# Two routings of a two-layer mixture-of-experts kernel: one-hot operands laid out with the token tile outermost

## The reference

```
# layer 0: 4 experts, each token goes to its best 2
probs = jax.nn.softmax(xf @ router_w + router_b, axis=-1)
top_p, top_i = jax.lax.top_k(probs, 2)
gates = zeros(T, e).at[arange(T)[:, None], top_i].add(top_p / sum(top_p))
out = einsum('te,etd->td', gates, expert_out)
# layer 1: 8 experts, each token goes to its best 1
route = jax.nn.sigmoid(x @ Wr + br)
max_ind, max_prob = argmax(route, axis=1), max(route, axis=1)
out = sum over e of (max_ind == e) * (gelu(x @ W1[e]) @ W2[e]), times max_prob
```

## Time and profile before

| | |
|---|---|
| median of 3 runs | 1730.97 us (1727.98 to 1731.4) |
| the profiled execution | 1730.75 us, its span 1729.0 us |
| mean granted TensorE clock | 0.928 |
| PE, DVE, ACT, POOL busy | 1521.6, 1123.6, 905.8, 1217.6 us |
| routing 0 stands at | about 414 to 437 us |
| routing 1 stands at | about 1486 to 1502 us |

### The profile page before, as it was taken

The page is one execution under the profiler, slowest core; times in us unless marked ns, Lnnn a source line. Parts: engine busy times, 40 slices in busy tenths (PEclk is TensorE's granted clock), DMA queues, the critical chain, the costliest instruction groups (busy, mean ns, idle before and its releaser), DMA issues.

```text
span 1729.0 us, 38207 instructions
## 1 busy us (share of the span) xinstructions
PE 1521.6 (88%) x13596; PEld 1140.2 (66%) x13596; DVE 1123.6 (65%) x1786; ACT 905.8 (52%) x2305; POOL 1217.6 (70%) x1024
## 2 busy tenths in 40 slices
PE   6799999986899999999999967777887767699998
PEld 5466665655788888888888843333333226599998
DVE  7888989887343433333445557999999998533333
ACT  6678787843343444343444345545555446354553
POOL 4757777732476676676778627999999996366664
PEclk9899999995799999999999977989999887599999
DMA  6014444418344445545465460011111255388885
GB/s 220 20 41 131 130 145 128 128 37 318 82 116 106 120 104 118 123 100 122 120 171 155 100 215 23 1 31 32 30 42 43 92 176 175 138 264 251 262 264 152
DMA packets 148049, 217.34 MB, mean 126 GB/s; under 512 B 48904, under 2 KB 108576, under 8 KB 142752
## 3 DMA queue, kind: packets, MB, share of 16 engines
q1 hardware_dynamic: 115296, 132.26, 23.7%
q0 software_dynamic: 32576, 82.63, 19.9%
HBM read 143.23 MB, written 71.61 MB: 124 GB/s over the span
## 4 chain that ended last, share of the span: by engine, by line
PE 58%; POOL 20%; DVE 9%; issue 5%; DMA 4%; ACT 1%; POOLq 0%; DVEq 0%; ACTq 0%; SPq 0%
PE ps L832 54%; POOL BIG L2575 17%; DVE BIG L1426 4%; DMA BIG<-HB,BIG 3%; PE ps L953 1%; DVE BIG L2059 1%; PE ps L1134 1%; POOL BIG L2760 1%; POOL BIG L2759 1%; DVE bnst L1433 1%; POOL XD L2749 1%; PE ps L1203 1%; DMA XD<-BIG 1%; ACT BIG L2108 1%; POOL BIG L2737 1%
## 5 line engine op out<-in xcount | busy, mean ns | idle before, releaser
L832 PE MATMUL ps<-BIG 128*128 128x256 f16 (+9 forms) x11168 | 1224.3, 284 | 125.0 <-DVE BIG L2037 49.2
L832 PEld LDWEIGHTS ps<-BIG 128*128 128x128 f16 (+3 forms) x11168 | 936.2, 100 | 383.3 <-DVE BIG L2037 76.3
L2575 POOL TENSOR_TENSOR BIG<-BIG 128x256 f16<-128x256 f32 (+7 forms) x550 | 730.4, 1457 | 211.4 <-ACT BIG L2108 200.1
L2108 ACT ACTIVATE BIG<-BIG 128x512 f16<-128x512 f32 (+3 forms) x527 | 318.0, 662 | 233.2 <-DVE BIG L1426 176.2
L1426 DVE TENSOR_TENSOR BIG<-BIG 128x512 f16<-128x512 f32 (+10 forms) x347 | 259.8, 758 | 209.5 <-ACT BIG L2108 165.0
L2108 ACT ACTIVATE BIG<-ps 128x64 f32<-128x64 f32 (+7 forms) x663 | 232.1, 424 | 194.6 <-PE ps L1134 108.0
L1426 DVE TENSOR_TENSOR BIG<-ps,BIG 128x512 f32<-128x512 f32 (+3 forms) x389 | 284.8, 809 | 14.5 <-PE ps L832 13.1
L1426 DVE TENSOR_TENSOR BIG<-BIG,ps 128x512 f32<-128x512 f32 (+2 forms) x147 | 94.9, 645 | 187.4 <-PE ps L832 168.1
L2059 DVE TENSOR_REDUCE BIG<-BIG 128x160 f32<-128x2560 f32 x64 | 186.0, 2906 | 0.0
L2749 POOL DMA_INDIRECT XD<-BIG x67 | 113.2, 1690 | 85.9 <-DVE BIG L1943 82.1
L2737 POOL DMA_INDIRECT BIG<-HB,BIG x106 | 109.7, 1035 | 50.6 <-issue 27.0
(11 more groups left out here) (176 smaller groups left out, 1025.4 us busy)
## 6 DMA issues: line engine op xcount, KB each, us to landing
WD<-BIG SPq DMA_DIRECT2D x80, 256.0 KB
BIG<-in_v SPq DMA_DIRECT2D x32, 512.0 KB
BIG<-in_w SPq DMA_DIRECT2D x24, 512.0 KB
BIG<-WD SPq DMA_DIRECT2D x32, 384.0 KB, 7.9
HB<-BIG SPq DMA_DIRECT2D x64, 128.0 KB, 2.5
WG<-BIG SPq DMA_DIRECT2D x32, 256.0 KB
BIG<-WD SPq DMA_DIRECT2D x16, 512.0 KB, 5.2
XD<-X SPq DMA_DIRECT2D x32, 128.0 KB, 2.4
```

The lines of the kernel that those rows point to most:

```text
L832: return e.matmul(o, lhsT, rhs, start=start, stop=stop, skip_group_check=True)
L2108: return e.activation(o, i, ACT.Copy)
L2575: return e.tensor_tensor(o, a, b, op)
```

## The change

Three ring buffers change their shape: the token tile, until now the innermost index, becomes the outermost. `S1` goes from [128, 8] to [8, 128], `A1` and `AP` from [2, NS, 8] to [8, 2, NS]. Each matmul now reads its 128 weights per partition and its 134 or 78 moving columns from adjacent addresses; until now two neighbours lay 8 elements (16 bytes) apart. The engines that write these buffers still go through the elements in the old order, with the eight token tiles innermost; the helper `by_tile` turns the output view, so the element after the next one written lies a whole row away (128 elements for `S1`, 2 x NS for `A1` and `AP`). `A0`, `lane8` and `tile8` and the other inputs keep their layout. Sizes, counts, waits and the order of instructions stay.

```diff
+def by_tile(ap):
+    return ap.rearrange("p r n -> p n r")
...
-                self.S1 = late.ring(4, 128, 8, dt=f16) if l else over.ring(3, 128, 8, dt=f16)
-                self.AP = late.ring(4, 2, NS, 8, dt=f16) if l else None
+                self.S1 = late.ring(4, 8, 128, dt=f16) if l else over.ring(3, 8, 128, dt=f16)
+                self.AP = late.ring(4, 8, 2, NS, dt=f16) if l else None
...
-                self.A1 = over.ring(3, 2, NS, 8, dt=f16)
+                self.A1 = over.ring(3, 8, 2, NS, dt=f16)
...
-                            m = mm(m_.mp, m_.S1[n % len(m_.S1)][:, :, r], m_.A1[n % 3][:, :, :, r], n == 0 and r == 0,
+                            m = mm(m_.mp, m_.S1[n % len(m_.S1)][:, r], m_.A1[n % 3][:, r], n == 0 and r == 0,
...
-                            m = mm(m_.pp, m_.S1[n][:, :, r], m_.AP[n][:, :, :, r], n == 0 and r == 0, n == 3 and r == 7)
+                            m = mm(m_.pp, m_.S1[n][:, r], m_.AP[n][:, r], n == 0 and r == 0, n == 3 and r == 7)
...
-                    tt(m_.S1[u % len(m_.S1)], bc(m_.s_lo[:, u // 4, 8 * (u % 4):8 * (u % 4) + 8], 1, 128), m_.lane8, ALU.is_equal).then_inc(s["rt"], 1)
+                    tt(by_tile(m_.S1[u % len(m_.S1)]), bc(m_.s_lo[:, u // 4, 8 * (u % 4):8 * (u % 4) + 8], 1, 128), m_.lane8, ALU.is_equal).then_inc(s["rt"], 1)
...
-                    tt(a1[:, 0], hot, bc(m_.tok[:, ch, g:g + 8], 1, NS), ALU.mult).then_inc(s["rt"], 1)
+                    tt(by_tile(a1[:, :, 0]), hot, bc(m_.tok[:, ch, g:g + 8], 1, NS), ALU.mult).then_inc(s["rt"], 1)
...
-                            tt(m_.AP[u][:, k], m_.A0[u], bc(p[:, 8 * u:8 * u + 8], 1, NS), ALU.mult).then_inc(s["rt"], 1)
+                            tt(by_tile(m_.AP[u][:, :, k]), m_.A0[u], bc(p[:, 8 * u:8 * u + 8], 1, NS), ALU.mult).then_inc(s["rt"], 1)
...
-                    e.activation(m_.A1[u % 3][:, 1], m_.A0[u % len(m_.A0)], ACT.Copy, scale=pcol[:, 0:1]).then_inc(s["a1_a"], 1)
+                    e.activation(by_tile(m_.A1[u % 3][:, :, 1]), m_.A0[u % len(m_.A0)], ACT.Copy, scale=pcol[:, 0:1]).then_inc(s["a1_a"], 1)
```

## The result

The changed kernel takes 1797.47 us in the median of its runs, against 1731.18 us for the kernel before in the same comparison: a ratio of 1.0389, 95% interval [1.037, 1.0407]. One run of the changed kernel took 3070.84 us; it stands apart from the other three (1795.81 to 1797.6 us) and is left out. The profiled execution took 1797.34 us with a span of 1795.6 us, 66.6 us more than before. I had forecast 1746 us with a range up to 1759: the sign was right, the time was outside the range.

A forecast was written before the change was run, and what follows sets the result against it. TensorE was taken as busiest (88%), its 64 matmuls on routing 0's path; slower VectorE writes would add 8.6 us in routing 0 and 6.15 in routing 1, +14.8, giving 1746 us, range 1733 to 1759.

The forecast's parts named there:

- What it costs VectorE: Both routings: strided writes cost 1.69 ns per element, bounds 1.05 and 2.33; S1 of 1024 elements 1.88 us, before 0.68.
- Rival 2: VectorE's strided writes: a two-byte write costs a read and a write, 2.33 ns per element; +28 us, 1759; chance 15%.
- TensorE's gain: Matmuls of both routings: packed operands cut a unit of eight to 0.92 us (from 1.97) and 0.54 (from about 1.18).
- (a): Routing 0: first three S1 and GpSimd's four additions take turns, each waiting for the other's running instruction; +3.6 us.
- (b): Routing 0: three pairs of one-hot and token product, 0.83 us apart before, 1.45 after.
- (c): Routing 0, units 3 to 7: period 3.14 us, TensorE needing 0.92 of it and waiting for VectorE.
- (d): End of routing 0: VectorE work that used to hide under TensorE's last units now stands open, 2.0 us.
- Routing 1: Routing of layer 1: line 1860 moves by +5.65 us, AP products add 2.9, the routing as a whole +6.15 us.
- ScalarE: ScalarE's part of 536 elements could grow from 744 ns to about 1.2 us, beside VectorE's 1.9 us, costing nothing.
- The clock: Dense work behind both routings: the clock's rise costs nothing new if it follows the work; at most 2 to 3 us.
- Rival 3: Both routings: VectorE keeps two elements per cycle and TensorE was all that counted; 1724.3 us; chance 7%.

The follow-up runs named there:

- m1: Kernel of single operations alone in different layouts, computing nothing of the reference; VectorE's 1024 two-byte results take 4703 ns at a step of 256 bytes, packed 692.
- e1: Changed kernel with A1 and AP put back as before, so only S1 is turned: 1776.36 us in one run, against 1734.95 for the kernel before.
- e2: Changed kernel with S1 put back as before, so only A1 and AP are turned: 1752.93 us in one run, +18 us.
- e5: Kernel before with only A1 and AP laid out in runs of four token tiles, S1 untouched: 1730.3 us against 1736.72, ratio 0.9967.
- e3: Kernel before with S1, A1 and AP all laid out in runs of four token tiles: 1728.04 us against 1734.95, ratio 0.9963.
- e4: Kernel before with S1, A1 and AP laid out in runs of two token tiles: 1733.55 us against 1736.72, ratio 0.9984.

## Why the prediction was wrong

The step that failed is the one under "What it costs VectorE": "I take 1.69, since TensorE's 16-byte step costs nearly the same per column; both ends are kept." The write costs 4.4 ns per element. Not only the value was wrong: the upper bound, 2.33, was too. I built it from float32 rows of another stride, charged twice, and m1 shows that these rows measure a different thing: a float32 word that hops costs 1.71 ns, a lone two-byte word 4.4. I found no row of a strided two-byte write in the trace of before, so 2.33 was a guess of a mechanism and bounded nothing. Rival 2 named the property that counts (the two-byte size), at half its price and at 15%; its reason, a read and a write back, is not shown: from 4 to 16 bytes the price grows with the step, which two fixed accesses would not give.

- **TensorE's gain.** 1.05 us per unit against 0.92 forecast, 0.70 against 0.54 in routing 1, both with a fixed part that I left out (about 0.15 us for each separated group). Right in kind. That the `S1` half of it is nothing, which e1, e2 and e5 show, I had not seen.
- **(a) Turns with GpSimd.** Right for GpSimd's side only. Its additions, from the groups of that stretch:

```profile
L2580 POOL TENSOR_TENSOR BIG<-BIG 128x268 f32<-128x268 f32 x1 | 4.5, 4452 | 0.1
L2580 POOL TENSOR_TENSOR BIG<-BIG 128x134 f32<-128x134 f32 x1 | 4.3, 4268 | 0.1
```

  They took 0.94 and 0.76 us before, and now each lasts nearly as long as the `S1` beside it. From the first `S1` to line 1827 it is 14.02 us, before 3.28: +10.7 where I had +3.6. But the three `S1` follow one another in 13.91 us, 4.6 each, so they hardly waited for an addition: turns as I had drawn them would have made it 15.4 at this price.
- **(b) Pairs.** TensorE's first groups stand 2.82 us apart (433.65 and 436.47); I had 1.45.
- **(c) Period.** The five groups from 446.29 to 475.28 stand 7.25 us apart; I had 3.14. VectorE's wait for TensorE is gone, as I said.
- **(d) Tail.** Line 1865 starts 1.87 us behind the last product (475.46 to 477.33); I had 2.0.

The stretches add up: 14.0 for the turns, 1.2 for the three conversions, 3 x 2.82, 5 x 7.25 and 1.9 are 61.8 us, where 62.2 were measured. That only says that no stretch is missing. The test of my steps is to put in the prices of m1 (4.70 us for an `S1`, 2.52 for a product of 536): they give 15.4, 1.2, 8.8, 37.2 and 2.0, 64.6 us. So the path and the overlaps of routing 0 were right to 2.4 us, more than half of it the turns, and the price of the write made up nearly all of the miss.

- **Routing 1.** +19.4 at line 1865 against +5.65, by the same price: four units of 4.0 + 1.15 are 20.7, less what TensorE gives back. Behind it, I had the last conversion and the second row fetch end at the same moment, 1507.05, each ready to hold TensorE. With the `AP` products at +8.7 us and not +2.9, the conversion (line 1897) comes last alone, and TensorE waits for it.
- **ScalarE** "costs nothing": in routing 0 that held, though at 2.68 and not 1.2 us, since VectorE's period was longer still.
- **The clock** gave a little over 1 us back, inside its term.
- **Rival 3** fell: below 0.9 ns the sign would have turned. e3 shows that its idea was sound (TensorE's 15.8 us are on the chain, and 5.9 of 6.05 us can be had), but only with writes that stay in runs; in runs of two it is 3.0 us (e4).

## What to carry to other kernels

Before a tile is turned for the engine that reads it, look at how its writer will step through it: the adjacent elements that are written together must stay adjacent, and a run of four two-byte elements was enough for VectorE's full speed here. What step the reader can bear depends on its clock: 8 bytes cost TensorE 1.14 against 1.08 us per unit at 0.50, and 120 against 57 ns per matmul at 1.00 (with both operands at 8 bytes, m1). Turn only the operand that gains by it (here the moving one, not the weights), and only as far as it gains. Where the trace has no row for an operation of this size of element, a bound built from rows of another size is no bound; widen the range by a factor, or measure the one operation first.

## What the runs showed of the hardware

- A two-byte result costs VectorE, with two sources, 0.28 ns per byte of step: 1.30 us for 1024 at 4 bytes, 2.43 at 8, 4.69 at 16 and no more beyond. In runs of two it is 1.03 us, in runs of four 0.69 as if packed. The Trainium skill, "SBUF — State Buffer", section "Door 1: The DMA port swizzle", says that accesses within one 16-byte line run at full bandwidth, so that up to 8 two-byte elements can be stepped over for free. For these writes the runs do not agree: the price begins at 4 bytes, and 16 bytes is where it stops rising.
- GpSimd and ScalarE pay about the same 4.7 us for 1024 at 256 bytes (4734 and 4743), from 2114 and 1056 packed.
- TensorE's moving operand at 16 bytes costs about twice the packed one at a clock of 0.50 (2.07 against 1.08 us per unit, e1 and the changed kernel), while weights at 16 bytes cost 0.03 us. In m1 at 1.00 a packed matmul of 128 columns takes 57 ns, 60 with the moving operand at 4 bytes and 120 with both at 8; with the moving one at 16 bytes it takes more than 200 at either level.
- A long VectorE instruction holds up GpSimd's indirect fetch as well. The first indirect fetch of weights in routing 1, which took 1.14 us before, has in the changed kernel's timeline

```profile
1541.10 4.43 POOL L2798 DMA_INDIRECT BIG<-WG,BIG  x1 [23.64 <-DVE BIG L1431]
```

- In routing 0 the granted clock was 0.50 throughout before, although TensorE was busy for 15.75 of 15.8 us there. With runs of four (e3) it rose to 1.00 in the middle of the routing, for about 3.5 us, and fell back. Two windows of e3, one ahead of the rise and one in it:

```profile
418.00:420.00 2.00, 1.11 (x10) 1.14 (x11) 1.93 (x5) 1.84 (x3) 0.00 (x0) 0.50 1.03 413
424.00:426.00 2.00, 1.74 (x13) 1.39 (x14) 2.00 (x6) 1.01 (x2) 0.00 (x0) 1.00 0.76 296
```

  So TensorE did not get the clock back while it was busy only with slow reads, and did with faster ones, though it was idle for part of the time. m1 shows the same without any gap: TensorE is busy throughout with reads at 16 bytes from 318.97 to 340.72, and the clock falls from 1.00 to 0.50 near 324 and stays there; it is back at 1.00 from 345, behind packed moving reads, and, after a second fall with reads at 16 bytes, from 376, behind reads at 8 bytes. In the changed kernel the reads are packed, but TensorE is busy for 9.47 of 47.3 us, and the clock stays at 0.50. VectorE sets the pace in that stretch of e3, so I put none of its gain down to this; that was not tested apart.
